# A sequence mixer and a mixture of experts on one core: the first batch in a new order, and the front of batch two beside the first routing

## The reference

```
z = x @ Wz;  B, C, dt, X = split(x @ Win)
delta = softplus(dt + dt_bias)
h_t = exp(-delta_t * exp(A_log)) * h_(t-1) + X_t (delta_t B_t);   y_t = h_t C_t + D * X_t
x1 = layernorm(x + (y * (silu(z) @ Wzg)) @ Wout)
dw1, dw2, dw3 = top-3 softmax of x1 @ P_w.T @ U1.T, U2.T, U3.T        # 12 experts
h = gelu(sum_e dw1[:, e] * x1 @ W1[e].T)
out = layernorm(x1 + sum_e dw2[:, e] * h @ W2[e].T + dw3 @ b2)
```

## Time and profile before

| | us |
|---|---|
| median of 3 runs (1656.87 to 1659.09) | 1657.14 |
| the profiled execution | 1658.27 |
| its span, first to last instruction | 1656.6 |
| TensorE busy | 1563.7 (94%) |
| VectorE busy | 1139.4 (69%) |
| GpSimd busy | 642.5 (39%) |
| ScalarE busy | 593.8 (36%) |
| granted TensorE clock, mean | 0.977 |

### The profile page before, as it was taken

How to read it: one execution, slowest core, us unless ns; L and a number is a source line. 1 busy time by engine, 2 the same in 40 slices (tenths; PEclk the granted TensorE clock), 3 DMA queues, 4 the chain that set the end, 5 groups by cost and what they waited for, 6 DMA issues and landing times.

```text
span 1656.6 us, 28375 instructions
## 1 busy us (share of the span) xinstructions
PE 1563.7 (94%) x8466; PEld 1242.3 (75%) x8466; DVE 1139.4 (69%) x3116; ACT 593.8 (36%) x1340; POOL 642.5 (39%) x734
## 2 busy tenths in 40 slices
PE   5459999999999999999999999999999999999997
PEld 3347878778787877778787787877778787787876
DVE  3636667686877768777676777767677776767644
ACT  4434242342424234242433424243342424424130
POOL 4526062352606336161533516144350623526040
PEclk9559999999999999999999999999999999999999
DMA  3513031220403113040321404022040412304020
GB/s 109 154 41 113 21 109 40 62 92 27 127 15 103 55 55 99 26 128 13 94 67 46 108 20 127 20 79 81 31 124 20 116 31 65 89 28 128 20 71 7
DMA packets 81311, 114.36 MB, mean 69 GB/s; under 512 B 10160, under 2 KB 36800, under 8 KB 81216
## 3 DMA queue, kind: packets, MB, share of 16 engines
q1 hardware_dynamic: 81216, 113.45, 23.8%
HBM read 108.28 MB, written 5.13 MB: 68 GB/s over the span
## 4 chain that ended last, share of the span: by engine, by line
PE 72%; issue 11%; POOL 9%; DVE 4%; ACT 2%; DMA 1%; POOLq 1%; DVEq 0%; SPq 0%; ACTq 0%
PE exp_bank L224 18%; PE exp_bank L226 17%; PE exp_bank L225 17%; PE mix_bank L723 4%; POOL sp_lo L938 4%; PE mix_bank L749 3%; PE mix_bank L731 3%; PE mix_bank L224 2%; PE mix_bank L226 2%; PE mix_bank L225 2%; POOL Wt L705 1%; ACT L424 1%; POOL sp_lo L521 1%; PE turn_bank L986 1%; PE mix_bank L831 1%
## 5 line engine op out<-in xcount | busy, mean ns | idle before, releaser
L938 POOL TENSOR_TENSOR sp_lo<-fbuf,sp_hi 128x512 fp32r<-128x512 f32 x192 | 247.3, 1290 | 255.9 <-ACT sp_hi L935 239.5
L224 PE MATMUL exp_bank<-sp_hi,w_hi 128*128 128x512 f32 x768 | 311.8, 406 | 15.9 <-DVE acc L1028 14.8
L224 PE MATMUL exp_bank<-w_hi,sp_hi 128*128 128x512 f32 x768 | 309.8, 403 | 2.0 <-POOL sp_lo L979 2.0
L225 PE MATMUL exp_bank<-w_lo,sp_hi 128*128 128x512 f32 x768 | 303.3, 395 | 0.0
L226 PE MATMUL exp_bank<-w_hi,sp_lo 128*128 128x512 f32 x768 | 303.2, 395 | 0.0
L226 PE MATMUL exp_bank<-sp_hi,w_lo 128*128 128x512 f32 x768 | 303.1, 395 | 0.0
L225 PE MATMUL exp_bank<-sp_lo,w_hi 128*128 128x512 f32 x768 | 301.5, 393 | 0.0
L935 ACT CAST sp_hi<-fbuf 128x512 fp32r<-128x512 f32 x192 | 119.0, 620 | 370.6 <-DVE fbuf L920 301.0
L1025 DVE SCALAR_TENSOR_TENSOR acc<-exp_bank,dw,acc 128x128 f32<-128x128 f32 x384 | 131.7, 343 | 124.9 <-PE exp_bank L226 123.8
L224 PEld LDWEIGHTS exp_bank<-sp_hi,w_hi 128*128 128x128 f32 x768 | 144.6, 188 | 67.6 <-POOL sp_lo L938 22.5
L705 POOL TENSOR_TENSOR Wt<-Wt,Gh 128x512 f32<-128x512 f32 x128 | 176.4, 1378 | 17.1 <-DVE Wt L698 17.1
(11 more groups left out here) (182 smaller groups left out, 2245.5 us busy)
## 6 DMA issues: line engine op xcount, KB each, us to landing
row_b<-dw_rows SPq DMA_DIRECT2D x192, 256.0 KB, 3.4
seg_b<-dA_rows SPq DMA_DIRECT2D x128, 256.0 KB, 3.7
ctd<-cum_rows SPq DMA_DIRECT2D x128, 96.0 KB, 3.3
x_in<-in_x SPq DMA_DIRECT2D x16, 256.0 KB, 2.8
result<-acc SPq DMA_DIRECT2D x16, 256.0 KB, 2.3
fbuf<-in_W1T SPq DMA_DIRECT2D x12, 256.0 KB, 3.5
fbuf<-in_W2T SPq DMA_DIRECT2D x12, 256.0 KB, 2.9
b_sb<-in_b SPq DMA_DIRECT2D x48, 0.5 KB
```

Source lines behind the costliest of these rows:

```text
L224: nc.tensor.matmul(ps, s_hi, m_hi, start=start and j == 0, stop=False)
L225: nc.tensor.matmul(ps, s_hi, m_lo, start=False, stop=False)
L938: sig("xw_lo", PO.tensor_tensor(sp_lo[:, at, :], wide[e % 2], sp_hi[:, at, :].bitcast(F32), ALU.subtract))
```

## The change

Everything is in `mixer_alone`, its setup, and the one `body` of batch one; the loop and what follows it are as before.

1. **Setup.** VectorE rounds only Win's B and C part first; Wz, the X part and Wzg follow behind the first transposes. Wzg's transfer is issued behind the small broadcast ones, and its high part is cast on ScalarE. The identity comes first on GpSimd. The 48 small transfers of b2 become four, later.
2. **Batch zero.** Rates, ends, all X tiles, the head copies 0 and 1 and the states stand ahead of the gate products. VectorE takes the rest of silu. `mix_y(q-1)` stands behind the scan of head 2q+1.
3. **Weight tiles.** Sixteen are split before the routing: VectorE takes the rest of tiles 0, 1, 3 and 5, GpSimd the other twelve. Tiles 16 to 19 are split during the routing, 20 to 22 early in batch one's body and 23 late in it, all on ScalarE and GpSimd, from other staging buffers.
4. **Batch one's front** (its x is loaded into `acc`): transposes, B and C, dt and step stand beside the first layer norm; z, silu, X, scores, rates, ends, zg and states behind the routing weights, all before the first expert product. Logits and the weights' transpose use expert banks.

```diff
@@ -45,6 +45,10 @@
     + [("out", "v", 1), ("lg", "lg", 1)]
 )
 MIX_USE = {u[0]: n for n, u in enumerate(MIX_USES)}
+MIX_FIRST = (
+    MIX_USES[:MIX_USE["X2"] + 1] + [("X3", "Xd", 4), ("st01", "state", 2), ("st2", "state", 3)]
+    + [(f"zg{q}", "zg", n + 1) for n, q in enumerate((1, 0, 3, 2))] + MIX_USES[MIX_USE["st2"] + 1:]
+)
...
+        st_wzg = Wt[:, 1, :].rearrange("p (k n) -> p k n", k=NK)
+
+        def round_rest(n, src, hi, lo):
+
+            DVE.tensor_copy(hi, src).then_inc(sems["chain"], 1)
+            DVE.wait_ge(sems["chain"], n)
+            DVE.tensor_tensor(lo, src, hi.bitcast(F32), ALU.subtract).then_inc(sems["cast"], 1)
...
+                SP.dma_start(st_wz, Wz[:, :]).then_inc(sems["wz"], 16)
...
+                SP.dma_start(st_wzg, Wzg.rearrange("(k p) n -> p k n", p=P)).then_inc(sems["wzg"], 16)
...
+                load_w(SP, range(RING))
+                SP.dma_start(wout[:, :, :], Wout.rearrange("(q p) n -> p q n", p=P)).then_inc(sems["small"], 16)
...
+            if eng is PE:
+                PE.wait_ge(sems["ident"], 2)
+            if eng is AC:
+                AC.preload_act_table_set(LOG_EXP)
+                AC.wait_ge(sems["pad"], 6)
...
+        def setup_z(eng):
+            if eng is DVE:
+                DVE.wait_ge(sems["wz"], 16)
+                round_rest(2, st_wz, wz_hi[:, :], wz_lo[:, :])
+                round_rest(3, st_win[:, 2 * NS + H:], wx_hi[:, :], wx_lo[:, :])
+            if eng is PE:
+                PE.wait_ge(sems["cast"], 1)
+                PE.wait_ge(sems["wbdt"], 2)
+
+        def setup_zg(eng):
+            if eng is AC:
+                AC.wait_ge(sems["wzg"], 16)
+                AC.activation(wzg_hi[:, :, :], st_wzg, ACT.Copy, scale=0.5).then_inc(sems["wzg_hi"], 1)
...
+                DVE.wait_ge(sems["wzg_hi"], 1)
+                DVE.scalar_tensor_tensor(wzg_lo[:, :, :], st_wzg, 0.5, wzg_hi[:, :, :].bitcast(F32),
+                                         ALU.mult, ALU.subtract).then_inc(sems["cast"], 1)
...
+        NW, RING, LATE = 2 * E, 4, 4
+        N1, NHP, LO_V = 16, 2, (0, 1, 3, 5)
+        late_slot = (0, 1, 2, 3, 0, 1, 4, 4)
+        late_stage = [Gh[0][:, :, :].rearrange("p c t -> p (c t)"),
+                      Gh[1][:, :, :].rearrange("p c t -> p (c t)"), seg_b[0][:, :], seg_b[1][:, :],
+                      acc[:, :, :].rearrange("p c d -> p (c d)")]
...
+        def split_w(eng, ks):
+
+            for k in ks:
+                _, hi, lo = w_tile(k)
+                at, landed, n = w_stage(k)
+                if k < NHP:
+                    if eng is DVE:
+                        DVE.wait_ge(landed, n)
+                        DVE.tensor_copy(hi, at).then_inc(sems["w_hi_v"], 1)
+                        DVE.wait_ge(sems["w_hi_v"], k + 1)
+                elif eng is AC:
+                    AC.wait_ge(landed, n)
+                    AC.copy(hi, at).then_inc(sems["w_hi"], 1)
+                if eng is (DVE if on_dve(k) else PO):
+                    if k >= NHP:
+                        eng.wait_ge(sems["w_hi"], k - NHP + 1)
+                    eng.tensor_tensor(lo, at, hi.bitcast(F32), ALU.subtract).then_inc(sems["w_lo1" if on_dve(k) else "w_lo0"], 1)
+                if k + RING < N1:
+                    load_w(eng, [k + RING])
...
             ahead = [4]
-            expert_split(eng, p, 0)
-            mix_scores(eng, b)
-            mix_silu_split(eng, b)
-            mix_rates(eng, b)
-            mix_ends(eng, b)
-            expert_prep(eng, p, 1)
+            if norm_before:
+                expert_split(eng, p, 0)
+                mix_scores(eng, b)
+                mix_silu_split(eng, b)
+                mix_rates(eng, b)
+                mix_ends(eng, b)
+            elif eng is PE:
+                wait(PE, "lg", p)
+                wait(PE, "dwT", p)
+            if norm_before:
+                expert_prep(eng, p, 1)
             expert_in(eng, p, 0)
-            mix_X(eng, b, [2])
             if norm_before:
+                mix_X(eng, b, [2])
                 expert_norm_stats(eng, p.prev())
-            mix_zg(eng, b)
-            mix_X(eng, b, [3])
-            if norm_before:
+                mix_zg(eng, b)
+                mix_X(eng, b, [3])
                 norm_root(eng, p.prev(), "ln2")
             expert_prep(eng, p, 2)
             expert_in(eng, p, 1)
             expert_prep(eng, p, 3)
-            mix_states(eng, b)
+            if norm_before:
+                mix_states(eng, b)
+            else:
+                split_w(eng, range(N1 + LATE, NW - 1))
+                load_w(eng, [NW - 1])
+                if eng is AC:
+                    AC.wait_ge(sems["w_lo0"], rests(NW - 2))
             mix_score_step(eng, b, 0)
             experts(eng, p, [2], ahead)
             mix_score_skip(eng, b, 0)
...
+            if not norm_before:
+                split_w(eng, [NW - 1])
...
         def mixer_alone(eng, b):
 
             mix_x(eng, b)
+            setup_z(eng)
             neg_a_ready(eng)
-            if eng is PE:
-                PE.wait_ge(sems["cast"], CASTS)
-                PE.wait_ge(sems["wbdt"], 2)
+            setup_zg(eng)
...
             mix_dt(eng, b)
-            mix_step(eng, b)
+            split_w(eng, range(0, 2))
+            if eng is PE:
+                PE.wait_ge(sems["cast"], 3)
+            mix_step(eng, b, table=False)
             mix_z(eng, b)
-            mix_silu_split(eng, b)
             mix_X(eng, b, range(2))
+            mix_silu_split(eng, b, on=DVE)
+            if eng is AC:
+                AC.preload_act_table_set(LOG_EXP)
             mix_scores(eng, b)
-            router_product(eng)
+            if eng is PE:
+                PE.wait_ge(sems["masks"], 6)
+                PE.wait_ge(sems["cast"], NCAST)
+            if eng in (SP, DVE):
+                eng.wait_ge(sems["zero"], 16)
             mix_rates(eng, b)
             mix_ends(eng, b)
-            mix_X(eng, b, [2])
-            mix_zg(eng, b)
-            mix_X(eng, b, [3])
-            split_expert_weights(eng, range(0, 4))
+            mix_X(eng, b, range(2, 4))
+            mix_score_step(eng, b, 0)
+            mix_score_step(eng, b, 1)
+            mix_score_skip(eng, b, 0)
+            mix_score_skip(eng, b, 1)
+            split_w(eng, range(2, 6))
+            router_product(eng)
             mix_states(eng, b)
-            mix_score_step(eng, b, 0)
-            mix_score_skip(eng, b, 0)
             mix_decay(eng, b, 0)
-            mix_score_step(eng, b, 1)
-            k = 4
+            mix_decay(eng, b, 1)
+            mix_zg(eng, b, range(0, 2))
+            mix_score_step(eng, b, 2)
+            mix_zg(eng, b, range(2, 4))
+            split_w(eng, range(6, 8))
+            nxt = Batch(None, 1)
+            k = 8
             for q in range(NQ):
                 mix_from_start(eng, b, q)
-                mix_score_skip(eng, b, 2 * q + 1)
-                mix_decay(eng, b, 2 * q + 1)
-                if q < NQ - 1:
-                    mix_score_step(eng, b, 2 * q + 2)
-                split_expert_weights(eng, range(k, k + 2))
+                if q > 0:
+                    mix_score_skip(eng, b, 2 * q + 1)
+                    mix_decay(eng, b, 2 * q + 1)
+                    mix_y(eng, b, q - 1)
+                    if q < NQ - 1:
+                        mix_score_step(eng, b, 2 * q + 2)
                 if q < NQ - 1:
                     mix_score_skip(eng, b, 2 * q + 2)
                     mix_decay(eng, b, 2 * q + 2)
                     mix_score_step(eng, b, 2 * q + 3)
-                mix_y(eng, b, q)
-                split_expert_weights(eng, range(k + 2, k + 4))
-                k += 4
-            split_expert_weights(eng, range(k, NW))
+                split_w(eng, [k])
+                k += 1
+            mix_y(eng, b, NQ - 1)
+            split_w(eng, range(k, N1))
+            if eng is SP:
+                SP.dma_start(acc[:, :, :], x_rows(nxt)).then_inc(sems["x_first"], 16)
+            late_free(eng)
+            load_w(eng, range(N1, N1 + LATE))
+            load_b2(eng)
             mix_out(eng, b)
-            expert_weights_ready(eng)
-            route_norm(eng, b)
+            if eng is PE:
+                PE.wait_ge(sems["router"], 1)
+            first_weights_ready(eng)
+            if eng is not DVE:
+                mix_x(eng, nxt, True)
+            route_stats(eng, b)
+            if eng is DVE:
+                mix_x(eng, nxt, True)
+            mix_bc(eng, nxt)
+            mix_dt(eng, nxt)
+            if eng is not DVE:
+                mix_step(eng, nxt)
+            route_scale(eng, b)
+            if eng is DVE:
+                mix_step(eng, nxt)
             mix_load_next(eng, b)
             route_transpose(eng, b)
             route_logits(eng, b)
-            nxt = Batch(None, 1)
-            mix_x(eng, nxt)
+            split_w(eng, range(N1, N1 + LATE))
+            if eng is SP:
+                wait(SP, "ps_xT", nxt)
```

(22 more changed lines are left out.)

315 lines of the change are left out of this document (168 added, 147 removed).

## The result

| | before | changed |
|---|---|---|
| median of the runs, us | 1657.0 (4 runs) | 1642.4 (4 runs, 1640.7 to 1642.7) |
| profiled execution, its span | 1658.3, 1656.6 | 1642.7, 1641.0 |
| first head pair of batch zero starts | 46.84 | 38.94 |
| x's sum of batch zero | 84.54 | 71.41 |
| routing weights ready | 102.07 | 92.83 |

The ratio is 0.9908 (0.989 to 0.9925): 14.6 us faster, where 19.6 were forecast. A second set of four runs of the changed kernel gave 1641.5 and 0.9901 (0.9886 to 0.9916).

What follows compares the result with a forecast made beforehand. Time was taken as the moment from which TensorE has no gap plus its work left then. Gains 10.9 + 8.5 + 2.5 - 2.2 = 19.7 off 1658.3 give 1638.6; median 1.1 lower, 1637.5, range 1630 to 1647.

Steps and rivals of the forecast that it cites:

- the likeliest case: Whole kernel: the forecast itself, median 1637.5 us, chance 0.50.
- rival A: Batch one's body: TensorE starves at experts 4 to 6, clock drops, 3 to 7 lost more, 1643; chance 0.15.
- Rival B: Engines block each other at four states operations, three start rows, two norms: 6.7 lost, 1644; chance 0.12.
- Setup to the rates: Batch zero's start: ScalarE's copies of B 3.8 earlier, at 10.4; rates' transfer 4.4 earlier, at 23.8.
- Rates to the first pair: Batch zero: first scan 8.7 earlier; `mix_y(0)` at 41.3, 5.5 earlier, with 24 gate products half cold ahead.
- The four turns: Batch zero's head pairs: scans beside products, SyncE's start rows late; `mix_out` at 67.2, 12.1 earlier.
- To the weights: Batch zero's last weight splits end at 69.3, ahead of `mix_out`'s end at 71.1; x's sum at 71.2, 13.3 earlier.
- Routing: x's sum to routing weights: top-3 at 84.5, then 6.1 unchanged; weights at 90.9, 11.2 earlier, 2.1 given back.
- Routing to expert 0: From weights, 15.4 before, gate products, an X tile and states run first; expert 0 at 106.5, 10.9 earlier.
- The 8.5 and 2.5 at expert 0: Batch one: 8.5 of mixer work already done before expert 0; 2.5 from its twelve products running warm.
- Body of batch one: Three late tiles on GpSimd delay expert 4's operand: TensorE waits 1.9, 0.3 more at expert 5, 2.2 lost.
- Rival D: Early gain does not arrive, only TensorE's moved work remains: about 8.8 gained, 1648; chance 0.06.

Runs made afterwards that it cites:

- e4: Changed kernel plus unread TensorE products behind batch zero's head pairs (fourteen after each of the first three, three after the last): 1638.6 us, 0.9884 of before.
- e5: Changed kernel with VectorE's start-row product in batch zero moved behind the scan of head 2q+1: 1635.7 us, 0.9867 of before.
- e1: Changed kernel with GpSimd's rests of tiles 16 to 19 moved behind batch one's silu split: 1639.9 us, 0.9898 of before.
- e2: Changed kernel with only the rests of tiles 18 and 19 moved behind batch one's silu split: 1639.3 us, 0.9889 of before.
- c2: c1 with tiles 20 to 22 transferred and split earlier, ahead of the operands of experts 2 and 3: 1628.9 us, 0.9829 of before.
- e6: Changed kernel with batch one's scores, silu, rates, ends, later X tiles, gate products and states back between its first experts: 1644.7 us, 0.9928 of before.
- e3: Changed kernel with ScalarE's head copies in batch one's body waiting only for their own buffer's rest, not all three: 1640.6 us, 0.9902 of before.
- c1: Changed kernel with e1, e3, e4 and e5 together, plus moved buffers and reloads for late tiles: 1629.7 us, 0.9838 of before.
- c4: c2 without the unread TensorE products in batch zero: 1632.1 us, 0.9839 of before.

## Why the prediction was right, and where it was not

The forecast for the total, 1637.5 with 1630 to 1647, holds the result, which is 4.9 above the forecast. The places and the order of the gains were those of the likeliest case; the total lies nearer to rivals A (1643) and B (1644), and a part of each came: a clock fall behind the wait at expert 4, and GpSimd's rests holding VectorE. By its steps:

**Setup to the rates:** right. B's copy at 9.18 (10.4 forecast), the rates' transfer at 22.88 (23.8).

**Rates to the first pair:** right. The pair of splits 3.49 (3.06), the pair of heads at 38.94 (41.3; the best case was 38.8). Of the 24 gate products about nine ran cold, not half.

**The four turns:** right by two errors. x's sum was forecast for 71.2 and came at 71.41. The turns were faster than my walk (`mix_out` at 65.47, not 67.2), and `mix_out` was 2.1 slower; that the two nearly cancel is luck. The pairs ran at the lower level before as well (3.45 for all four; now for the last three). But before, the clock had risen by `mix_out` (0.50 in the last pair, 1.00 in it), and now it had not (0.50 and 0.63); the walk priced it by that row of before, and e4 shows that this is what the 2.1 are. The chain named was right, start rows issued late by SyncE behind the wait for tile 12 (landed by 50.23, forecast 51.8). e5 adds what they held: VectorE's start-row product, with a skip and a scan queued behind it.

**To the weights:** right. The last rest ended at 67.3 and held nothing.

**Routing:** the step that failed. "Top-3 starts at 84.5": it started at 83.63. "Its own 6.1 to the weights stay": they became 9.2, because GpSimd's four rests held VectorE's comparisons (e1, e2). Rival B named this mechanism and put it at the states, start rows and norms, for 6.7 in all. There it took 1.6: 0.2 and 0.9 on two start-row products and 0.5 on one state operation of batch one, nothing on the norms. The place where it struck hardest, two-input operations on the routing's path beside four rests in a row, was not in its list. ScalarE's table loads cost 1.28 each and nothing behind, as charged: the load at 74.15 is followed by work at 75.45. The Trainium skill ("SBUF — State Buffer", Who interferes with whom) says of a VectorE operation with two SBUF inputs and a GpSimd one that the second waits for the whole first; by that rule, the three measured doses agree: each comparison that meets a rest ends 0.16 or 0.17 behind it.

**Routing to expert 0:** right. 14.4 from weights to expert 0 (15.6), at full clock.

**The 8.5 and 2.5 at expert 0:** they came, in this accounting: 17.3 at batch two is 10.2 for the start, 8.5 and 2.5, less 2.2 for the wait and 1.7 behind it. c2, with neither the wait nor the fall, bears out the 11.0: 144.9 from expert 0 to batch two's sum, where before's 155.7 less 11.0 is 144.7. As the worth of one part of the change they would be misread, as e6 shows.

**Body of batch one:** right in size (2.2 forecast, 2.17 measured) and cause: e3 shows ScalarE's wait on the last of three rests. The forecast had no term for the clock's fall behind it, which rival A had: 1.2 by e2, 1.8 by nine matmuls 0.2 slower.

**Rival D's sum:** short of its own condition. 8.8 is 8.5 + 2.5 - 2.2; the 2.1 of the longer routing path, which it names, would leave 6.7, near 1650 and outside the range. Nothing of D came.

Sum: 19.7 forecast, 15.6 measured between the spans. Expert 0 0.7 less (the weights 1.9 late, the way from them 1.2 shorter), the body 1.7 less, of which e2 puts 1.2 on the clock, the last batch 2.2 less, the loop 0.5 more: 4.1.

Open: whether anything in the change makes the last batch's fall likelier; why the front's length varies by 2.3. The record places that variation, without its cause: from the first pair to x's sum the six profiles take 32.4 to 32.6, and they differ ahead of it, by up to 1.4 at the rates' transfer (22.3 to 23.75) and by 0.7 behind it in e1 and e6, where three more of the 24 gate products ran at the lower level.

## What to carry to other kernels

Work moved to GpSimd beside the routing held three of VectorE's operations with two SBUF inputs here, each until the GpSimd instruction beside it ended. Look for such operations on the path row by row, and put the work behind them. On an in-order engine, ask of every operation that waits for a transfer what is queued behind it: moving one such operation behind a scan shortened batch zero's turns by 2.6 to 3.3. Price each short piece of TensorE work behind a wait at both clock levels, and take the difference into the range. When edits are put together, compare their stretches and not the total alone: c1's total came out as the sum of four gains that overlapped, with a clock fall elsewhere that happened not to come.

## What the runs showed of the hardware

A wait of 2.2 us on TensorE at a granted clock of 1.00 is followed by a fall to the lower level in some executions and not in others, with the same instructions around it: at expert 4 in four profiles (waits of 2.17 to 2.22) and not in four others (1.89 to 2.40), in the last batch in eight profiles of thirteen that have the wait. The length of the wait does not sort them: 2.40 in e1 had no fall. A fall lasts some 3 us; it cost 1.2 at expert 4 and 1.6 or 2.2 in the last batch. With pairs of 28 short matmuls and waits of 1.8 to 6.1 us between them, `mix_out` took 3.84 in e5 and 5.46 in c4. The Trainium skill ("TensorE: Matmul & The Clock Gate", What's actually happening) says that the point at which the clock changes shifts with where in the gate's own cycle the work falls; it tells this of the rise at a kernel's start. That the falls here come or not for the same reason fits these runs, but none tests it. A VectorE comparison of 128x144 with both inputs in SBUF takes 0.30 alone, and 1.25 to 1.36 beside GpSimd operations of 128x512 that take 1.3.
